# A decoder layer on one core: head sums by a matrix product, and another order of cross attention, its end and the feed-forward

## The reference, cut to what matters

```python
x = x + attn(layernorm(x), W_qkv)                       # one causal head
x = x + xattn(layernorm(x), ctx, ctx, mask, Wq, bq, ..., Wo, bo)
x = x + ffn(layernorm(x), w_gate, w_up, w_down)

# xattn: H = 16 heads of D_K = 8
scores = einsum('bhqd,bhkd->bhqk', q, k) / sqrt(D_K)     # masked keys: -1e9
p_attn = softmax(scores, axis=-1)
x = einsum('bhqk,bhkd->bhqd', p_attn, v)
return merge_heads(x) @ Wo.T + bo

# ffn: act_qdq rounds to 16-bit levels with ONE scale, the largest |value| of the whole tensor
x = act_qdq(x); up = act_qdq(x @ Wup.T); gate = act_qdq(x @ Wgate.T)
sig = fixed_qdq_u16(sigmoid(gate)); gate = act_qdq(gate * sig)
o = act_qdq(gate * up); return o @ Wdown.T
```

## Time and profile before

| what | value |
|---|---|
| median of 3 runs | 376.21 us (368.89, 376.21, 377.52) |
| the profiled execution | 369.51 us, its span 367.7 us |
| PE, DVE, ACT, POOL busy | 308.6, 282.1, 248.0, 177.7 us |
| cross attention: first VectorE maxima, last | 88.5 us, 217.2 us |
| costliest group on VectorE | L1331 maxima, 64 of 1219 ns |

### The profile page before, as it was taken

One profiled execution on the slowest core, in us unless ns is written; L12 is line 12 of the kernel. 1 busy time (PEld: TensorE's weight loads), 2 busy tenths in 40 slices (PEclk: granted clock), 3 DMA queues, 4 the chain that ended last, 5 costly groups with the idle time before them and its releaser, 6 DMA issues.

```text
span 367.7 us, 9555 instructions
## 1 busy us (share of the span) xinstructions
PE 308.6 (84%) x3621; PEld 204.2 (56%) x3621; DVE 282.1 (77%) x589; ACT 248.0 (67%) x452; POOL 177.7 (48%) x321
## 2 busy tenths in 40 slices
PE   3999999997599998989889899689987668660996
PEld 2697877774366665656556566434432223220996
DVE  5369988876767878888887885858779967897563
ACT  3368888875358787778778776268697736991850
POOL 3559999973313474755666471100058841662000
PEclk9999999999759999999999999889998998895699
DMA  5961666665640000000000000000000000000034
GB/s 139 299 193 32 200 206 205 200 206 160 213 133 2 5 2 4 4 3 4 2 4 4 4 4 2 0 0 0 2 0 1 0 0 0 1 0 0 18 98 116
DMA packets 23751, 22.67 MB, mean 62 GB/s; under 512 B 3545, under 2 KB 21402, under 8 KB 23578
## 3 DMA queue, kind: packets, MB, share of 16 engines
q1 hardware_dynamic: 22170, 21.78, 19.5%
q10 hardware_dynamic: 1536, 0.28, 0.4%
HBM read 15.75 MB, written 6.31 MB: 60 GB/s over the span
## 4 chain that ended last, share of the span: by engine, by line
PE 41%; DVE 22%; POOL 17%; issue 8%; ACT 7%; DMA 2%; SPq 1%; ACTq 1%; POOLq 0%; DVEq 0%
DVE mxs L1537 8%; PE banks L834 7%; PE banks L655 7%; PE banks L874 7%; PE banks L616 4%; DVE nm L1331 4%; POOL rstd L352 3%; PE banks L677 3%; POOL X L448 3%; POOL pickd L371 2%; PE banks L673 2%; PE banks L668 2%; PE banks L621 2%; DMA k_dram<-klo 2%; PE banks L536 2%
## 5 line engine op out<-in xcount | busy, mean ns | idle before, releaser
L1331 DVE TENSOR_REDUCE nm<-banks 128x8 f32<-128x1024 f32 x64 | 78.0, 1219 | 21.7 <-PE banks L612 21.7
L1028 ACT ACTIVATE PT<-banks,bmask,vmask 128x1024 f32<-128x1024 f32 x64 | 76.8, 1200 | 2.1 <-PE banks L621 2.1
L834 PE MATMUL banks<-X3T,upT 128*128 128x512 f32 x96 | 48.9, 660 | 15.4 <-DVE mxs L1537 9.4
L484 POOL TENSOR_TENSOR G<-ng,sq 128x1536 int32<-128x1536 int32 (+3 forms) x9 | 26.1, 2903 | 43.6 <-DVE sq L1562 43.6
L1537 DVE TENSOR_REDUCE mxs<-G 128x1 f32<-128x1536 int32 (+4 forms) x27 | 41.9, 1566 | 6.7 <-ACT G L1064 6.7
L655 PE MATMUL banks<-PT,VP 128*32 128x128 f32 x1024 | 43.0, 287 | 0.4
L834 PEld LDWEIGHTS banks<-X3T,upT 128*128 128x128 f32 x96 | 19.1, 208 | 43.4 <-issue 20.6
L908 ACT ACTIVATE h<-X,shift,rstd 128x128 f32<-128x128 f32 x64 | 26.4, 482 | 13.9 <-POOL shift L397 13.8
L655 PEld LDWEIGHTS banks<-PT,VP 128*32 128x32 f32 x1024 | 25.7, 112 | 8.1 <-issue 0.7
L1016 ACT ACTIVATE oT<-banks 128x128 f32<-128x128 f32 x32 | 8.9, 277 | 30.9 <-PE banks L673 30.9
L433 POOL CAST NM<-nm 128x64 bf16<-128x64 f32 x32 | 7.6, 238 | 43.8 <-DVE nm L1331 43.8
(11 more groups left out here) (183 smaller groups left out, 710.8 us busy)
## 6 DMA issues: line engine op xcount, KB each, us to landing
kd<-k_dram SPq DMA_DIRECT2D x32, 128.0 KB, 2.7
qd<-q_dram SPq DMA_DIRECT2D x32, 128.0 KB, 2.5
ctxg<-in_ctx_dram SPq DMA_DIRECT2D x8, 256.0 KB, 3.2
X3T<-m_dram SPq DMA_DIRECT2D x1, 1792.0 KB, 10.1
out_dram<-y SPq DMA_DIRECT2D x7, 256.0 KB, 2.3
X<-in_x_dram SPq DMA_DIRECT2D x3, 512.0 KB, 10.0
k_dram<-khi SPq DMA_DIRECT2D x8, 128.0 KB, 1.8
k_dram<-klo SPq DMA_DIRECT2D x8, 128.0 KB, 2.2
```

The lines of the kernel that those rows point to most:

```text
L834: m = pe.matmul(bank(2 + FC * (g % 2) + k), w[:, k * P:k * P + P], grp(X3T, g), start=True, stop=True)
L1028: act.activation(PT[:, a, :], bank(2 + 2 * a, 2), ACT.Exp, bias=bmask[:, n:n + 1], scale=vmask[:, n:n + 1]).then_inc(S["t_exp"], 1)
L1331: V.tensor_reduce(nm[:, n % 2, 2 * NSET * a:2 * NSET * (a + 1)], bank(0, 2).rearrange("p (h m) -> p h m", m=P), AX.X, ALU.max, negate=True ...
```

## The change

**Cross attention.** The two transposes of `queries` are gone. In their place one product with a constant matrix `heads_` (`sums`, 128 x 128 by 128 x 256) copies each head's sum into all 16 rows of that head. `attend` then takes one reciprocal of those 128 x 256 values, and multiplies the 128 x 256 values of `oun` by them. The result still has the heads down the partitions, so `turn` and `turn_copy` are gone, and the projection is two products (`project`), one for each half, with Wo spread over the 16-row heads (`WOE`, turned once into `WOT` in the first stretch: one DVE copy, two transposes on PE, one ACT copy, one DVE memset).

**Its order.** On PE the scores of queries stand before those of keys in each set of four, the semaphore for DVE is raised after the last of them, and `maxima_in` follows. On ACT `out_copy` stands ahead of `project_copy`. On DVE the statistics stand between the two maxima, and `largest3` is taken for two sequences at a time. At the end four of the six group copies of X3T (L1431, 128 x 512 each) and one of three weight copies move from DVE, so that ACT has six group copies and two weight copies.

**Feed-forward.** The product of the last group of the sigmoid pass is made by POOL in two halves, where DVE made one of them. The scale after the up pass is split: its transpose stands on PE one group earlier, and the last quantisation of the sigmoid stands between its two halves on DVE. At the end of the gated product two reductions move ahead of the last product.

The diff, cut to what the text speaks of:

```diff
@@
-        orec = sb("orec", [P, H], where=early)
+        WOE = sb("WOE", [P, 2 * P], where=early)
+        WOT = sb("WOT", [P, 2, P], where=early)
+        heads_ = sb("heads_", [P, P], where=early)
+        orec = sb("orec", [P, 2 * P], where=early)
         oun = sb("oun", [P, 2 * P], where=early)
-        on_ = sb("on_", [P, P], where=early)
+        on_ = sb("on_", [P, 2 * P], where=early)
-        oT = sb("oT", [P, P], where=early)
@@ gpsimd
-            level_product(NG - 1, slice(0, PB), NG + 1)
+            for h_ in range(2):
+                level_product(NG - 1, slice(h_ * PB, (h_ + 1) * PB), NG + 1)
@@ tensor
+            def turn_output_weights():
+                pe.wait_ge(S["w_oe"], 2)
+                for a in range(2):
+                    m = pe.transpose(bank(3)[:, a * P:(a + 1) * P], WOE[:, a * P:(a + 1) * P], ident[:, :])
+                m.then_inc(S["w_ot"], 1)
@@
             def scores(n, a):
                 for s in range(NSET):
                     for k in range(2):
+                        m = score_q(n + 3, s, 2 * (1 - a) + k)
+                    if s == NSET - 1:
+                        m.then_inc(S["t_sn"], 1)
+                    for k in range(2):
                         score_k(n + 1, s, 2 * a + k)
-                    for k in range(2):
-                        m = score_q(n + 3, s, 2 * (1 - a) + k)
-                m.then_inc(S["t_sn"], 1)
-                maxima_in(n + 1, a)
@@
-            def queries(n):
+            def sums(n):
                 pe.wait_ge(S["t_ou"], n + 1)
+                pe.matmul(bank(6 + n % 2)[:, 2 * P:4 * P], heads_[:, :], oun[:, :], start=True, stop=True).then_inc(S["t_den"], 1)
+
+            def project(n):
+                pe.wait_ge(S["t_o"], n + 1)
                 for a in range(2):
-                    m = pe.transpose(bank(6 + n % 2)[:, (2 + a) * P:(3 + a) * P], oun[:, a * P:(a + 1) * P], ident[:, :])
-                m.then_inc(S["t_tr"], 1)
-
-            def turn(n):
-                pe.wait_ge(S["t_o"], n + 1)
-                pe.transpose(bank(6 + n % 2)[:, 0:P], on_[:, :], ident[:, :]).then_inc(S["t_oT"], 1)
-
-            def project(n):
-                pe.wait_ge(S["t_oTc"], n + 1)
-                pe.matmul(bank(6 + n % 2)[:, P:2 * P], oT[:, :], WXT[:, 3, :], start=True, stop=True).then_inc(S["t_wo"], 1)
+                    m = pe.matmul(bank(6 + n % 2)[:, P:2 * P], on_[:, a * P:(a + 1) * P], WOT[:, a, :],
+                                  start=(a == 0), stop=(a == 1))
+                m.then_inc(S["t_wo"], 1)
@@ cross(n)
                 if n + 1 < B:
                     max_rows(n + 1)
+                if n > 0:
+                    sums(n - 1)
...
                 pv(n, 0)
-                if n > 0:
-                    queries(n - 1)
...
                 both(n, 0)
-                if n > 0:
-                    turn(n - 1)
                 pe.wait_ge(S["t_exp"], 2 * n + 2)
                 pv(n, 1)
@@
-                if g == 1:
+                if g == 0:
                     over_partitions(3, 1, 0)
@@ scalar, for n in range(B)
                 probs(n, 0)
+                if n > 0:
+                    out_copy(n - 1)
                 if 1 < n < B - 1:
                     project_copy(n - 2)
-                if n > 0:
-                    out_copy(n - 1)
                 if n + 1 < B:
                     max_copy(n + 1)
                 probs(n, 1)
-                if n > 0:
-                    turn_copy(n - 1)
+                if n == B - 1:
+                    rows3_copy(0, 2)
+                    rows3_copy(1, 3)
@@ vector
+            by_head = [P, P // VW, VW]
+            V.tensor_copy(heads_[:, :].rearrange("p (h c) -> p h c", c=VW),
+                          bc(ident[:, :].rearrange("p (h c) -> p h c", c=VW)[:, :, DK:DK + 1], by_head)).then_inc(S["c_wz"], 1)
@@
             def attend(n):
-                dve.wait_ge(S["t_tr"], n + 1)
-                wait(dve, "t_o", n)
-                o3 = bank(6 + n % 2)[:, 2 * P:4 * P].rearrange("p (h c) -> p h c", c=VW)
-                V.reciprocal(orec[:, :], o3[:, :, DK]).then_inc(S["t_rec"], 1)
+                dve.wait_ge(S["t_den"], n + 1)
+                wait(dve, "t_wo", n)
+                V.reciprocal(orec[:, :], bank(6 + n % 2)[:, 2 * P:4 * P]).then_inc(S["t_rec"], 1)
                 dve.wait_ge(S["t_rec"], n + 1)
-                wait(dve, "t_oT", n)
-                V.tensor_tensor(on_[:, :].rearrange("p (h e) -> p h e", e=DK), o3[:, :, 0:DK],
-                                bc(orec[:, :].unsqueeze(2), [P, H, DK]), ALU.mult).then_inc(S["t_o"], 1)
+                V.tensor_tensor(on_[:, :], oun[:, :], orec[:, :], ALU.mult).then_inc(S["t_o"], 1)
@@ for n in range(B)
                     attend(n - 1)
-                for k in range(2):
-                    if n + 3 < B:
-                        maxima(n + 3, k)
-                if g > 1 and b == 1:
-                    dve.wait_ge(S["u_x3"], GB * (g - 1))
-                    largest3(g - 2, g - 2, (0, GB))
...
+                if n + 3 < B:
+                    maxima(n + 3, 0)
+                if 1 < n < B - 1:
+                    stat3(n - 2)
                 if g > 0 and b == 1:
                     aggregate3(g - 1)
+                if g > 1 and b > 1:
+                    k = b - 2
+                    dve.wait_ge(S["u_x3"], GB * (g - 2) + 2 * k + 2)
+                    largest3(g - 2, 2 * (g - 2) + k, (2 * k, 2 * k + 2))
+                if n + 3 < B:
+                    maxima(n + 3, 1)
@@ sigmoid pass
                 sigmoid_levels(g, slice(0, FW), g + 2)
+                if g == NG - 1:
+                    scales_from(2, 3, 0)
                 silu_largest(g - 1)
...
                 if g == NG - 2:
                     dve.wait_ge(S["b_umx"], NG)
-                    scales(2, 3, 0)
+                    row_maxima(2, 3)
@@ gated product, g = NG - 1
+            dve.wait_ge(S["c_od"], NG - 1)
+            product_largest(g - 1, g - 1, slice(PC, FW))
+            dve.wait_ge(S["c_op"], NG - 1)
+            product_largest(g - 1, g, slice(0, PC))
...
+            product(g, PL)
```

More of the change, by code:

```diff
@@ L736, in _ @@
             scores_k(0, 0)
+            maxima_in(0, 0)
             pe.wait_ge(S["t_max"], 4)
@@ L768, in turn_early_rows3 @@
                     pe.wait_ge(S["u_x3"], GB * (g + 1))
-                    wait(pe, "u_tc", g - 1)
+                    if g in (2, 3):
+                        pe.wait_ge(S["u_tc"], g - 1)
+                    if g in (4, 5):
+                        pe.wait_ge(S["u_tca"], g - 3)
                     turn_rows3(k, g)
@@ L990, in _ @@
                     turned_weights()
+                if i == 1:
+                    act.wait_ge(S["w_ot"], 1)
+                    act.activation(WOT[:, :, :].rearrange("p a d -> p (a d)"), bank(3)[:, 0:2 * P], ACT.Copy
+                                   ).then_inc(S["w_otc"], 1)
                 if live(i - 3):
@@ L1009, in out_copy @@
                 act.wait_ge(S["t_pv"], 2 * n + 2)
-                wait(act, "t_tr", n)
+                wait(act, "t_o", n)
                 act.activation(oun[:, :], bank(6 + n % 2)[:, 0:2 * P], ACT.Copy).then_inc(S["t_ou"], 1)
-            def turn_copy(n):
-                act.wait_ge(S["t_oT"], n + 1)
-                wait(act, "t_wo", n)
-                act.activation(oT[:, :], bank(6 + n % 2)[:, 0:P], ACT.Copy).then_inc(S["t_oTc"], 1)
             def project_copy(n):
@@ L1464, in _ @@
                 row3(NG - 2, b)
-            for k in range(2):
-                rows3_copy(k, 2 + k)
-            dve.wait_ge(S["u_xd"], GB)
-            largest3(NG - 2, NG - 2, (0, GB))
-            weights_copy(0, gateT, 2)
             residual(B - 2)
@@ L1473, in _ @@
             attend(B - 1)
-            weights_copy(1, upT, 3)
+            weights_copy(0, gateT, 2)
+            largest3(NG - 2, 2 * NG - 4, (0, GB))
+            residual(B - 1)
+            stat3(B - 1)
+            aggregate3_last(GB - 1, GB)
             dve.wait_ge(S["u_rstd"], NG)
@@ L1477, in _ @@
                 row3(NG - 1, b)
-            residual(B - 1)
-            stat3(B - 1)
-            aggregate3_last(GB - 1, GB)
-            dve.wait_ge(S["u_xd"], 2 * GB - 1)
-            largest3(NG - 1, NG - 1, (0, GB - 1))
-            for k in range(2):
-                rows3_copy(k, 4 + k)
             dve.wait_ge(S["u_rstd"], NG + 1)
@@ L1497, in next_units, with row_maxima @@
                     n_unit[0] += 1
-            def scales(k0, k1, where):
+            def row_maxima(k0, k1):
                 n_scale[0] += 1
@@ L1505, in scales, with scales_from @@
                 V.tensor_copy(mxw[:, 0:w, :], bc(mx1[:, r].unsqueeze(2), [P, w, P])).then_inc(S["g_mx"], 1)
+            def scales_from(k0, k1, where):
+                n, r, w = n_scale[0], slice(k0, k1), k1 - k0
                 dve.wait_ge(S["g_all"], n)
@@ L1518, in scales @@
```

(3 more changed lines are left out.)

108 lines of the change are left out of this document (59 added, 49 removed).

## The result

The changed kernel takes **395.8 us** (median of 4 runs, 394.98 to 396.27), the kernel before 372.55 us in the four runs shown (367.21 to 377.52): a ratio of 1.075, 95% interval [1.071, 1.079]. The ratio compares fast runs alone, which leaves out the 376.21 and 377.52 us of the kernel before. The profiled execution took 395.69 us, its span is 393.9 us, 26.2 us more than before. It is slower, as forecast; the time lies 7 us under the forecast of 403 us, and only 0.8 us inside the low end of the range; one of the four runs, 394.98 us, lies just outside it.

The account below looks back on a forecast made before the run. The bound was taken to change by stage; in cross attention, DVE's maxima and PE's scores alternate. 369.5 + 33.8 (sequences) + 1.7 (end) - 3.0 (feed-forward) + 0.4 (start) = 402.4, taken as 403 us; 8-in-10 range 395 to 418.

Parts of the forecast that it names:

- The sequence: Cross attention, DVE's loop: 5.2 us a sequence instead of 3.95, for 27 sequences, +33.8 us.
- my line: DVE reciprocal in `attend`: 144 ns + 6.5 ns a column from four narrow widths, 1.81 us for 256 columns.
- my 0.05 for two SBUF operands: Cross attention, product until first maxima: 0.05 us added because both operands are now in SBUF and may slow the product.
- The start: First stretch: two transposes, two copies and one memset added, +0.4 us, from 0 to 1.
- The end of cross attention: Last maxima to first global maximum: four longer `attend` +6.9 us, partly offset by moved copies and idle time, +1.7 us.
- Feed-forward: Sigmoid pass and scale -2.3 us, gated product -0.7 us; together -3.0 us, between -1 and -4.
- The cheap reciprocal: Rival, DVE in `attend`: columns beyond the 36th cost about one cycle, reciprocal 0.54 us, total 360 to 366 us; 6 in 100.
- The steeper one: Rival, DVE reciprocal: 8.3 ns a column, 2.2 us for 256, total 410 to 420 us; 15 in 100.
- Late sums: Rival, cross attention: DVE waits for `t_den` 0.1 to 0.4 us each sequence, total 405 to 413 us; 12 in 100.
- PE's clock: Rival, cross attention: holes keep PE at 1.2 GHz, about 6 us a sequence, +22 us, total 425 us; 5 in 100.
- PE's share: Sign to look for: PE's busy share of the cross attention stage falls to some 70%.
- The floor without the reciprocal: Total if the reciprocal were cheap: PE's loop decides, near 3.75 us a sequence, 360 to 366 us.

Follow-up runs that it names:

- run 1: Changed kernel with the reciprocal over only 16 of its 256 columns, the others left at ones: 353.15 us, ratio 0.954 against the kernel before.
- run 2: Changed kernel with a copy of the same 128 x 256 from PSUM in place of the reciprocal: 351.5 us in one run.
- run 4: Changed kernel with the reciprocal over 128 of its 256 columns, the others left at ones: 371.7 us, ratio 1.0085 against the kernel before.
- run 7: Changed kernel with the old order of scores (keys, then queries) and the semaphore behind the last: 397.7 us, ratio 1.077 against the kernel before.
- run 9: Changed kernel with the last step of each scale (`lev`, 128 x 1) as TENSOR_SCALAR instead of TENSOR_TENSOR: 395.3 us, ratio 1.071 against the kernel before.
- run 3: Changed kernel with reciprocals of 16 to 512 columns, from SBUF and PSUM, added at the program's end: 6.25 ns a column, 1.70 us for 256.
- run 10: Kernel before, plus the change's end of cross attention and feed-forward, largest values for two sequences at a time, and run 9's edit: 361.5 us, ratio 0.981.

## Why the prediction was right, and where its sizes were off

**The mechanism held.** DVE's reciprocal is a straight line in its width, it lies on the path in every sequence, and PE gets the idle time. Narrow it and 42.7 us go (run 1); put a copy in its place and 44 go (run 2); halve it and 24 go (run 4). The size came out 7 us too high. Part of that nearness is luck: I had left out a term (below) that by my own prices is 1.7 us, and with it the forecast would have been nearly 9 us too high.

**The sequence, 5.2 us forecast, 5.01 measured.** Term by term: maxima to reciprocal 1.14, as predicted; reciprocal to product 1.78, not 1.84 (the reciprocal took 1.75, and my line gave 1.81); product to maxima 0.35, not 0.39, so that my 0.05 for two SBUF operands was not needed; first to second maxima 1.71 to 1.75, not 1.80. In this last gap DVE waits 0.29 us, where it waited 0.63: the statistics fill 0.28 us of it, and the gap itself is 0.1 us shorter. PE stands idle for 0.43 us ahead of these scores, as shown above, so it can start them as soon as the maxima have been read. Run 7 has the same 1.73 us with the old order of scores, so that the earlier semaphore isn't what did it. These four make 0.16 us, the rounding up to 5.2 another 0.03: 27 x 0.19 = 5.1 us. That is the whole miss of the stage, +28.7 where I had +33.8, and most of the miss of the total.

**The start** came 2.0 us earlier. 1.33 us of it are already there at the first maxima of self attention (15.88 us, and 17.21 before). In other traces with the changed kernel's start these begin at 15.4 to 17.5 us, so this differs from run to run. My +0.4 us for the added transposes can't be told from that.

**The end of cross attention**: +1.3 us behind the last maxima, against 1.7. But I left out a term: there are 28 `attend`s before the last maxima, not 27, and the one more costs +1.5 us. It stood in neither of my sums.

**Feed-forward**: -3.3 against -3.0, by other parts than I thought. From the maxima `mxa` of one scale to the next: the sigmoid pass 35.08 us where it was 36.88, and the short last piece 6.60 where it was 7.32, together -2.5 (I took -2.3; the slow `lev` had cost 0.9 of it, as run 9 shows). The gated product 27.41 where it was 28.97: -1.6, twice my 0.7. Down: -0.65. Against these the gate pass, which the change doesn't touch, was 1.4 us longer in this run (28.24; 26.82 before, 26.99 in run 9), at a granted clock of 0.88, where both others had 0.94. So that my -3.0 came out is in part luck: the other passes gave -4.7.

**The rivals.** The cheap reciprocal is excluded by runs 1 to 3, and so is the Trainium skill's 1.04 ns a column plus 75 ns ("Vector Engine (DVE) Microarchitecture Reference", section Measured stream behaviour on trn2) for this operation: it makes 342 ns for 256 columns, and run 3 has 1696. The copy of 256 columns, 411 ns, is near it. The steeper one, worked out as eight times that column from the repeat count of 8 in the Trainium skill ("VectorE: DVE Perf Modes", section Walkthrough: the 8-slice pipeline in each mode), is excluded by run 3: 6.25 ns, six columns' worth and not eight. Late sums: DVE idles 3.6 us before all 32 reciprocals together, and 3.3 of these are the first one and two at the end. In the kernel before, the waits ahead of its 32 reciprocals came to 5.7 us. PE's clock did fall for a while, and shows how much slack was there:

```profile
160.00:170.00 10.00, 7.48 (x180) 5.05 (x174) 9.60 (x15) 6.48 (x10) 4.36 (x12) 1.00 0.01 2
170.00:180.00 10.00, 8.62 (x174) 5.74 (x172) 9.76 (x13) 6.26 (x10) 5.59 (x14) 0.83 0.01 2
```

```profile
181.51 1.76 DVE L1415 RECIPROCAL orec<-banks 128x256 f32<-128x256 f32 x1 [0.16 <-PE banks L675]
```

From 170 to 200 us the granted clock was 0.83 on average, between the levels of 1.2 and 2.4 GHz, after 60 us at full speed in which PE was busy for 7.5 of every 10 us. PE grew to 8.6 of 10, and DVE waited 0.16 us in a sequence where `sums` took 1.16 us instead of 0.65. In the next one `sums` took 0.65 again, so that 0.83 is a mean of both levels. Three sequences cost 5.20 to 5.25 us and not 4.99, 0.7 us together: this rival is real, and cheap here. Late sums cost nothing that the kernel before had not paid.

**What I would have seen with more care.** PE's share was to fall to some 70%, and it fell to 78% (75% where the clock was full). The floor without the reciprocal was to be 360, and is 352 us: PE's own time in a sequence is 3.6 us, not 3.75. So the change without the width of its reciprocal is 4 to 5% under the kernel before, and this is what makes the wide reciprocal dear: about 43 us, not 26.

## What to carry to other kernels

A layout that saves transposes by repeating a value down the partitions also repeats every operation on it. Price that operation at the new width from its own rows: four narrow widths of the same operation gave the wide one within 4% of what it takes in the kernel, while a copy or a product of that width would have been wrong by four times. Time such a change in pieces, too: its end and its feed-forward, with run 9's edit, are worth 2% on the old heads (run 10), while the change as a whole costs 7.5%.
